# Graph hops that gather with one f32 product per item, with build steps placed inside the hops

## The chip, the cores and the metric

One core of a Trainium2 chip runs the whole program. The metric is device time in microseconds from start to end of one execution; smaller is better. The engines are TensorE (PE, matmul; its weight loads are listed as PEld and its sequencer as PEldq), VectorE (DVE), ScalarE (ACT), GpSimd (POOL) and SyncE (SP, which issues DMAs).

## The reference, cut to what matters

A graph has 3125 nodes with 128 features and 100000 edges, sorted by destination. Layer 0 is an attention layer with five hops; layer 1 is three graph convolutions.

```python
# layer 0: a[e, head] is the softmax share of edge e at its destination node
f = feat0
for _ in range(HOP):                                   # HOP = 5
    msg = f[src] * a[:, :, None]
    agg = jax.ops.segment_sum(msg, dst, num_segments=n)
    f = (1.0 - ALPHA) * agg + ALPHA * feat0
...
# layer 1: three times
h = x @ W
out = jax.ops.segment_sum(h[src_a] * norm[:, None], dst_a, num_segments=n) + b
```

Two things are computed around the change. A *hop* reads the row of each edge's source node, weighs it by the edge's eight head shares, and sums it at the destination. The *adjacency* for layer 1 is built once as a dense table in DRAM, `adj`, from the edges' weights.

## The kernel before, in words

Nodes are cut into 25 buckets of 125. The edges of one (destination bucket) or of one (source bucket, destination bucket) pair are cut into items of up to 128 edges; four items make a group.

**Hop 0** runs over 51 iterations of four groups. For each group SP loads rows that an earlier stage left in DRAM, VectorE makes the destinations' one-hot (L1402) and weighs the rows (L1449), and TensorE adds them up per bucket in PSUM with two products for each item, one for the rows and one for the weights' sum (L1062, L1065). From iteration 8 (`BUILD_FROM`) on, one **build step** goes with each group. A step is four items of the adjacency: VectorE writes a place factor (L1409) and four key factors (L1413), TensorE multiplies them into cells in PSUM bank 7 (`build_cells`, L1049), VectorE adds the cells to a running sum (`build_sums`, L1425), and SP stores four rows of it to `adj` (`store_step`, L690). There are 352 steps; 172 are done in hop 0, and **180 in loops of their own behind it** (L1294, L1706, L1983).

Beside hop 0 GpSimd writes one record for each edge to DRAM, sorted by bucket pair (L869). Behind the 180 steps comes the **record stage**: GpSimd gathers the records, 128 items at a time, eleven times (L880), and TensorE turns them (`turn_records`, L1071). It leaves the shares in `ex_it`, the destinations in `dst_c`, and the sources, as bf16, in DRAM (`ids_d`). GpSimd's first gather waits for all record DMAs and for the sums of hop 0.

**Hops 1 to 4** each run over 352 groups, in 44 iterations of eight. The rows of the current node table `na` stay in SBUF, and a group goes like this:

- SP loads the sources of two groups at a time, the same row into all 125 partitions (L717), into a ring of four.
- VectorE compares them with the partition's number, which gives the source one-hots in bf16 (`compare_sources`, L1455).
- TensorE gathers: one-hot times the rows of the item's source bucket, into bank 7 (`gather_items`, L1112). The table is kept as three bf16 parts, so an item takes three bf16 matmuls that add up in PSUM.
- VectorE weighs bank 7 into `msg` (`weigh`, L1472) and makes the next group's destination one-hot (`dst_onehots`, L1462).
- TensorE scatters: destination one-hot times `msg`, added to the destination bucket in banks 0 to 6 (L1103), in f32. An f32 product shows as two weight loads and two matmuls.

TensorE's order is written out in `cell_pass` (L1084): for group k it loads the bucket numbers of gather k+1 and of scatter k into registers (`cell_regs`, L553, four at a time), waits for the weigh of group k, issues gather k+1, then scatter k. There is one bank for the gathered rows, so gather k+1 cannot start before weigh k has read it.

Between hops VectorE adds `feat0` to the banks (`hop_sums`, L1977), ScalarE and VectorE **split** the new table into its three bf16 parts (`split_parts`, L985, and `split_rest`, L1488), and TensorE clears banks 0 to 6 (L1041). The feed-forward part of layer 0 and the three convolutions follow.

Semaphores set all of the order. Every engine's and SP's instructions run in the order in which they are written, so whatever stands behind a wait waits too.

Of the kernel before, what the change touches and what calls it, by code (L numbers as in the profile page):

```python
# [12 lines left out]
P = 128  # L13
# [40 lines left out]
BUILD_FROM = 8  # L54
BUILD_AFTER = STEPS - (ITERS - BUILD_FROM) * SLOTS
# [5 lines left out]
assert SLOTS == 2 * BSLOTS and BG * NB * WN <= BANK and BUILD_AFTER % SLOTS == 0 < BUILD_AFTER  # L61
# [16 lines left out]
MASKS = 12  # L78
# [10 lines left out]
PARTS_F = 3  # L89
# [5 lines left out]
HALF = ITEMS // 2  # L95
assert ITEMS % 2 == 0 and HALF <= BANK
# [17 lines left out]
def gnn_stack(nc, a, out):  # L114
    ctx = ExitStack()
    with ctx:
# [38 lines left out]
        src_it = sb("src_it", [P, KB * P], I32)  # L155
        dloc = sb("dloc", [P, KB * P])
        w_it = sb("w_it", [P, KB * P])
# [6 lines left out]
        pidx = sb("pidx", [P, 1])  # L164
        dump_at = sb("dump_at", [P, 1])
# [135 lines left out]
        def tail_part(n):  # L301
# [16 lines left out]
        idb = gap_f[:, 0:PK * P // 2].bitcast(BF16).rearrange("p (k e) -> p k e", e=P)  # L318
        dst_rows = gap_f[:, PK * P // 2:PK * P // 2 + 2 * P].rearrange("p (s e) -> p s e", s=2)
        ids_at = PK * P // 2 + 2 * P  # L320
        ids = gap_f[:, ids_at:ids_at + PRING * LOAD * P // 2].bitcast(BF16).rearrange("p (s n) -> p s n", s=PRING)
        assert ids_at + PRING * LOAD * P // 2 <= L // 2 + 1
        dst_c = raw[:, 0:PITEMS]
        cell_row = x_sb.rearrange("p b f -> p (b f)")[0:1, 0:2 * PITEMS].bitcast(I32)
        split_at = 2 * NB * F
        split = U[:, split_at:split_at + PARTS_F * NB * F // 2].bitcast(BF16).rearrange("p (k b f) -> p k b f", k=PARTS_F, f=F)
        assert 2 * PITEMS <= NB * F and PARTS_F * NB * F // 2 <= (NB + 1) * F + NB * BN
        rec_in = ga_flat[:, 0:2 * P * REC].rearrange("p (s e c) -> p s e c", s=2, c=REC)
        msg = ga_flat[:, 0:PRING * G * F].rearrange("p (s g f) -> p s g f", s=PRING, g=G)
        src_t = ga_flat[:, PRING * G * F:PRING * G * F + PRING * LOAD * P // 2].bitcast(BF16).rearrange(  # L330
            "p (s i e) -> p s i e", s=PRING, e=P)
        rest = ga_flat[:, 0:BANKS * BANK].rearrange("p (s n) -> p s n", s=BANKS)
# [200 lines left out]
        def group_of(s, r, k):  # L533

            return r * PSTEPS + ((s - 1) * PGROUPS + k)

        def load_of(s, r, q):

            return r * PRING + ((s - 1) * PLOADS + q)
# [1557 lines left out]
```

## Time and profile before

| | us |
|---|---|
| median of 2 runs (8714.96 to 8715.48) | 8715.22 |
| the profiled execution, its own time | 8704.12 |
| its span, first to last instruction | 8702.4 |

| engine | busy us | share of the span |
|---|---|---|
| PE (matmul) | 6495.1 | 75% |
| PEld (weight load) | 5400.2 | 62% |
| DVE | 4864.4 | 56% |
| POOL | 1744.7 | 20% |
| ACT | 406.5 | 5% |

The mean granted clock of TensorE is 0.811 of 2.4 GHz; in a stretch it is mostly 0.50 (1.2 GHz) or 1.00. Shares are means over stages with different limits, so each stage has to be read by itself. Matmuls are pipelined, their ends are modelled, and a busy PE is not a PE at its peak. "issue" is idle time in which the engine waited for nothing that the profile shows. Times in rows count from the span's start.

### The profile page before, as it was taken

What the parts mean: (1) busy time and instruction counts of PE and PEld (TensorE: products, weight loads), DVE (VectorE), ACT (ScalarE), POOL (GpSimd) and SP (SyncE); (2) the same over time, 40 slices, a digit from 0 to 9 for tenths busy, and PEclk for the clock granted to TensorE, in tenths of its full rate; (3) what the DMA queues carried; (4) which work ended last, traced back from release to release, by engine and by line L of the source; (5) the groups of instructions that cost most, each with busy time, mean ns of one, the idle gap of its engine ahead of it and who ended that gap; (6) DMA issues with size and microseconds to landing.
All of it is one profiled execution on the core that took longest, in us unless ns stands there. A gap on an engine that the chain in (4) does not pass through costs nothing.

```text
span 8702.4 us, 162184 instructions
## 1 busy us (share of the span) xinstructions
PE 6495.1 (75%) x41703; PEld 5400.2 (62%) x41704; DVE 4864.4 (56%) x9329; ACT 406.5 (5%) x1487; POOL 1744.7 (20%) x1671
## 2 busy tenths in 40 slices
PE   4455464599994445888888888888888888888599
PEld 2344353599994444666666666666666666666499
DVE  7888577788887776444444444444444444444411
ACT  0111111100000000000000000000000000000100
POOL 0677575477774000000000000000000000000000
PEclk9565555555555556999999999999999999999899
DMA  2344643234432222111111111101111111111276
GB/s 59 116 138 133 131 141 98 57 106 106 107 105 68 62 62 79 39 39 39 39 39 37 39 39 39 39 37 39 39 39 39 38 39 39 39 39 39 78 271 241
DMA packets 546072, 646.43 MB, mean 74 GB/s; under 512 B 84553, under 2 KB 393084, under 8 KB 536029
## 3 DMA queue, kind: packets, MB, share of 16 engines
q1 hardware_dynamic: 475380, 520.58, 18.4%
q0 software_dynamic: 67216, 120.62, 5.1%
q10 hardware_dynamic: 3418, 4.48, 0.2%
q8 instruction: 32, 0.52, 0.0%
q14 instruction: 26, 0.21, 0.0%
HBM read 487.75 MB, written 158.90 MB: 74 GB/s over the span
## 4 chain that ended last, share of the span: by engine, by line
PE 67%; issue 14%; DVE 11%; POOL 3%; DMA 2%; DVEq 1%; ACT 1%; SPq 1%; POOLq 0%; ACTq 0%; PEldq 0%; PEld 0%
PE ps L1112 27%; PE ps L1103 17%; PE ps L1049 7%; PE ps L1065 6%; PE ps L1358 5%; POOL U L821 3%; DVE gap L1425 3%; PE ps L1062 2%; PE ps L1227 1%; PE ps L1220 1%; DVE U L1933 1%; DVE U L1905 1%; DMA U<-tab_he,stage 1%; DVE gap L1413 1%; DVE gap L1541 1%
## 5 line engine op out<-in xcount | busy, mean ns | idle before, releaser
L1112 PE MATMUL ps<-U 125*128 x16896 | 2354.7, 228 | 821.0 <-issue 792.5
L1112 PEld LDWEIGHTS ps<-U 125*128 125x128 bf16 x16896 | 1628.5, 96 | 1626.0 <-issue 1085.6
L1472 DVE TENSOR_TENSOR U<-ps,ex_it 128x512 f32<-128x512 f32 x1408 | 976.5, 694 | 2538.2 <-PE ps L1112 2538.2
L1103 PE MATMUL ps<-U 128*125 128x128 f32 x11264 | 1608.4, 284 | 0.0
L1103 PEld LDWEIGHTS ps<-U 128*125 128x125 f32 x11264 | 1346.6, 187 | 45.1 <-issue 0.2
L1049 PE MATMUL ps<-gap 128*128 128x125 f32 x2816 | 695.2, 425 | 402.2 <-DVE gap L1425 402.2
L821 POOL DMA_INDIRECT U<-tab_he,stage x806 | 843.7, 1047 | 525.0 <-issue 243.5
L1462 DVE TENSOR_TENSOR U<-raw,iota_p 128x500 f32<-128x500 f32 x1408 | 944.4, 671 | 0.0
L1049 PEld LDWEIGHTS ps<-gap 128*128 128x128 f32 x2816 | 635.1, 330 | 448.8 <-issue 448.8
L869 POOL DMA_INDIRECT rec_d<-ex_it,stage x806 | 847.4, 1051 | 245.5 <-issue 228.8
L1425 DVE SCALAR_TENSOR_TENSOR gap<-gap,U,ps 128x125 f32<-128x125 f32 x1408 | 487.2, 346 | 273.8 <-PE ps L1049 100.4
L1065 PE MATMUL ps<-U 128*125 128x128 f32 x1632 | 628.1, 489 | 0.0
L1227 PE MATMUL ps<-U 125*128 x1632 | 402.4, 424 | 217.3 <-ACT U L930 216.4
L1227 PEld LDWEIGHTS ps<-U 125*128 125x128 f32 x1632 | 345.5, 313 | 274.9 <-issue 274.9
L1220 PE MATMUL ps<-ident,U 128*125 128x128 f32 x816 | 225.6, 428 | 334.8 <-DVE U L1402 319.7
L1062 PEld LDWEIGHTS ps<-w_it,U 128*125 128x125 f32 x1632 | 444.5, 333 | 5.8 <-issue 5.8
L1065 PEld LDWEIGHTS ps<-U 128*125 128x125 f32 x1632 | 443.1, 332 | 0.0
L1220 PEld LDWEIGHTS ps<-ident,U 128*125 128x125 f32 x816 | 186.4, 313 | 370.1 <-DVE U L1402 347.8
L1413 DVE TENSOR_SCALAR gap<-iota_p,U,raw 128x125 f32<-128x125 f32 x1408 | 388.7, 356 | 0.0
L1062 PE MATMUL ps<-w_it,U 128*125 x1632 | 344.3, 280 | 4.2 <-DVE U L1449 4.2
L1455 DVE TENSOR_SCALAR U<-gap,pidx 125x1024 bf16<-125x1024 bf16 x704 | 339.1, 482 | 0.1
L1402 DVE TENSOR_TENSOR U<-dloc,iota_p 128x500 f32<-128x500 f32 x409 | 282.5, 691 | 86.1 <-DMA U<-edge_fe 53.4
(323 smaller groups left out, 3604.4 us busy)
## 6 DMA issues: line engine op xcount, KB each, us to landing
gap<-ids_d SPq DMA_DIRECT2D x704, 250.0 KB
adj<-gap SPq DMA_DIRECT2D x1408, 64.0 KB
edge_fe<-U SPq DMA_DIRECT2D x204, 256.0 KB, 2.5
U<-edge_fe SPq DMA_DIRECT2D x204, 256.0 KB
ex_it<-adj SPq DMA_DIRECT2D x30, 1600.0 KB, 6.1
U<-adj SPq DMA_DIRECT2D x30, 1600.0 KB, 6.1
fe_a<-adj SPq DMA_DIRECT2D x15, 1600.0 KB, 6.1
U<-tab_he,stage POOLq DMA_INDIRECT x806
```

Of the source, the lines that this page charges most:

```text
L821: pool.indirect_dma_start(to[:, k, j, :], None, table, bass.IndirectOffsetOnAxis(ap=stage[:, k, j:j + 1], axis=0)).then_inc(got[k], 16)
L869: pool.indirect_dma_start(rec_d, bass.IndirectOffsetOnAxis(ap=stage[:, k, j:j + 1], axis=0), recs[:, k, j, :], None).then_inc(got[k], 16)
L1049: mm = nc.tensor.matmul(cells_at(j), hot_p[:, k % BSLOTS, j, :], prod[:, k % BSLOTS, j, :], start=True, stop=True)
L1062: nc.tensor.matmul(ps[0:BN, bass.ds(b + W_SUMS, 1)], hot[:, k, j, :], w_it[:, bass.ds(r * PER_ITER + (k * G + j), 1)], start=False, stop=F ...
L1065: mm = nc.tensor.matmul(ps[0:BN, bass.ds(b * F, F)], hot[:, k, j, :], ga[:, k, j, :], start=False, stop=False, skip_group_check=True)
L1103: mm = nc.tensor.matmul(ps[0:BN, bass.ds(b * F, F)], dst_hot[:, k % PRING, j, :], msg[:, k % PRING, j, :], start=False, stop=False, skip_g ...
L1112: mm = nc.tensor.matmul(bank(7)[:, j * F:(j + 1) * F], src_t[0:BN, k // 2, k % 2 * G + j, :], split[0:BN, n, bass.ds(b, 1), :].rearrange(" ...
L1220: t = nc.tensor.transpose(bank(k % 2)[0:BN, j * P:(j + 1) * P], hot[:, k, j, :], ident[:])
L1227: mm = nc.tensor.matmul(bank(2 + k % 2)[:, j * F:(j + 1) * F], hot_t[:, k % 2, j, :], nb_pad[0:BN, bass.ds(b, 1), :].rearrange("p b f -> p ...
L1425: ins = v.scalar_tensor_tensor(out=win_acc[:, u, j, 0:CELL], in0=before, scalar=win_same[:, bass.ds(win_item(t, r, k, j), 1)], in1=cells_a ...
L1462: v.tensor_tensor(dst_hot[:, (k + ahead) % PRING], dst_c[:, bass.ds(r * (PSTEPS * G) + (k + ahead) * G, G)].unsqueeze(2).to_broadcast([P, ...
L1472: v.tensor_tensor(msg[:, k % PRING].rearrange("p g (h d) -> p (g h) d", h=HEADS), bank(7).rearrange("p (x d) -> p x d", d=HD), by, ALU.mul ...
```

## The change

1. The three bf16 parts and the split are gone. The gather is one f32 product for each item, with source one-hots in f32, in a ring of two loads instead of four.
2. The source one-hots move from VectorE to ScalarE, as two dependent activations: |source - partition|, then relu(1 - that).
3. The bucket numbers are interleaved in `cell_row` (three small loads instead of one), and TensorE reads eight for each group with one register load.
4. Builds begin at iteration 7 of hop 0 (176 steps there). The loops of 180 steps are gone; the other 176 steps go into hops 1 to 4, one for each eight groups. In group 4 (`CELL_AT`) TensorE builds cells in bank 7 between weigh 4 and gather 5, and ScalarE copies them out (`cells_kept`). VectorE does the rest in pieces: the place factor in group 0, key factors in groups 1 and 2, sums in groups 5 and 6.
5. SP stores a step's four rows in the next iteration, behind the first of its four loads of sources.

Some buffers move; the ids rings now lie in spare places of other tiles.

```diff
-BUILD_FROM = 8
-BUILD_AFTER = STEPS - (ITERS - BUILD_FROM) * SLOTS
+BUILD_FROM = 7
+STEPS_0 = (ITERS - BUILD_FROM) * SLOTS
+SRING = 2
+CELL_AT = 4
...
+            def load_ids(s, r, q):
+                sp.wait_ge(src_hots, load_of(s, r, q) + 1)
+                sp.dma_start(ids[q][0:BN, :], ids_d[bass.ds(r * (PRING * LOAD * P) + q * LOAD * P, LOAD * P)]
+                             .partition_broadcast(BN)).then_inc(loaded[q], 16)
+
             for s in range(1, HOPS):
-                with sp.Fori(0, PITERS) as r:
-                    for q in range(PRING):
-                        sp.wait_ge(src_hots, load_of(s, r, q) + 1)
-                        sp.dma_start(ids[0:BN, q, :], ids_d[bass.ds(r * (PRING * LOAD * P) + q * LOAD * P, LOAD * P)]
-                                     .partition_broadcast(BN)).then_inc(loaded[q], 16)
+                for r0, r1 in cut(0, 1, PITERS):
+                    with sp.Fori(r0, r1) as r:
+                        load_ids(s, r, 0)
+                        if s > 1 or r0:
+                            store_step(r * BG + (STEPS_0 + (s - 1) * PITERS - 1) * BG, step_of(s, r) + 1, 1)
+                        for q in range(1, PRING):
+                            load_ids(s, r, q)
+            store_step((STEPS - 1) * BG, STEPS + 1, 1)
...
-            act.wait_ge(built, 1)
...
+            def compare_sources(s, r, q, ahead=0):
+
+                use = (q + ahead) % PRING
+                to = src_t[0:BN, use % SRING].rearrange("p i e -> p (i e)")
+                act.wait_ge(loaded[use], r * 16 + 16 * (ITERS + (s - 1) * PITERS + 1 + (q + ahead) // PRING))
+                act.wait_ge(gathered, 2 * load_of(s, r, q + ahead) + 2)
+                nc.scalar.activation(to, ids[use][0:BN, :], ACT.Abs, bias=below[0:BN, 0:1]).then_inc(src_apart, 1)
+                act.wait_ge(src_apart, load_of(s, r, q + ahead) + 1)
+                nc.scalar.activation(to, to, ACT.Relu, bias=ones[0:BN, 0:1], scale=-1.0).then_inc(src_hots, 1)
+
+            for s in range(1, HOPS):
+                compare_sources(s, 0, 0)
+                for r0, r1 in cut(0, PITERS - 1, PITERS):
+                    with act.Fori(r0, r1) as r:
+                        for q in range(PRING):
+                            if q == PRING - 1:
+                                act.wait_ge(cell_sums, step_of(s, r) + 1)
+                                nc.scalar.copy(cells_kept, bank(7, BG * CELL)).then_inc(cells_out, 1)
+                            if not (r0 and q == PRING - 1):
+                                compare_sources(s, r, q, 1)
...
             def cell_pass(s):
-                pe.wait_ge(split_done, BANKS * s)
                 pe.wait_ge(src_hots, (s - 1) * PLOADS + 1 + PRING)
-                gather_items(0, cell_regs(pe, 0))
+                gather_items(0, cell_regs(pe, 2 * PITEMS, G))
...
-                            of = None if last else cell_regs(pe, i + G)
-                            to = cell_regs(pe, i + PITEMS)
+                            v_ = cell_regs(pe, i + G, G) if last else cell_regs(pe, i, 2 * G)
 
                             pe.wait_ge(weighted, group_of(s, r, k) + 1)
+                            if k == CELL_AT:
+                                build_cells(step_of(s, r), 0)
+                                scatter_items(s, r, k, v_[-G:])
+                                pe.wait_ge(cells_out, r + ((s - 1) * PITERS + 1))
                             if not last:
                                 if k % 2:
                                     pe.wait_ge(src_hots, load_of(s, r, (k + 1) // 2) + (1 + PRING))
-                                gather_items((k + 1) % PSTEPS, of)
+                                gather_items((k + 1) % PSTEPS, v_[0:G])
+                            if k != CELL_AT:
+                                scatter_items(s, r, k, v_[-G:])
...
             def gather_items(k, cells):
 
                 for j, b in enumerate(cells):
-                    for n in range(PARTS_F):
-                        mm = nc.tensor.matmul(bank(7)[:, j * F:(j + 1) * F], src_t[0:BN, k // 2, k % 2 * G + j, :],
-                                              split[0:BN, n, bass.ds(b, 1), :].rearrange("p b f -> p (b f)"),
-                                              start=(n == 0), stop=(n == PARTS_F - 1))
+                    mm = nc.tensor.matmul(bank(7)[:, j * F:(j + 1) * F], src_t[0:BN, k // 2 % SRING, k % 2 * G + j, :],
+                                          na[0:BN, bass.ds(b, 1), :].rearrange("p b f -> p (b f)"), start=True, stop=True)
                 mm.then_inc(gathered, 1)
...
+            def build_in_hop(s, r, k):
+
+                item = r * BG + (STEPS_0 + (s - 1) * PITERS) * BG
+                if k == 0:
+                    place_factor(item, 0)
+                if k in (1, 2):
+                    ins = key_factors(item, 0, (2 * k - 2, 2 * k - 1))
+                    if k == 2:
+                        ins.then_inc(prod_ready, 1)
+                if k == CELL_AT + 1:
+                    dve.wait_ge(cells_out, r + ((s - 1) * PITERS + 1))
+                    dve.wait_ge(acc_out[1], r * (16 * BG) + 16 * BG * (STEPS_0 // BSLOTS + (s - 1) * PITERS + 1))
+                if k in (CELL_AT + 1, CELL_AT + 2):
+                    lanes = (0, 1) if k == CELL_AT + 1 else (2, 3)
+                    add_cells(item, step_of(s, r), 1, 1, lanes, lambda j: cells_kept[:, j * CELL:(j + 1) * CELL])
...
             def cell_pass(s):
-                compare_sources(s, 0, 0)
                 dst_onehots(s, 0, 0)
...
-                            if k % 2 == 0 and not (r0 and k == PSTEPS - 2):
-                                compare_sources(s, r, k // 2, 1)
                             weigh(s, r, k)
                             if not (r0 and k == PSTEPS - 1):
                                 dst_onehots(s, r, k, 1)
+                            build_in_hop(s, r, k)
...
-            with dve.Fori(0, BUILD_AFTER // SLOTS) as r:
-                for k in range(SLOTS):
-                    build_factors(STEPS - BUILD_AFTER, r, k)
-                    build_sums(STEPS - BUILD_AFTER, r, k - 1)
-            build_sums(STEPS, 0, -1)
-            dve.sem_inc(built, 1)
+            build_sums(ITERS, -1)
...
             for n in range(1, HOPS):
-                split_rest(n - 1)
                 cell_pass(n)
```

## Rows read from the trace of the kernel before

**Rows 1.** The page's chain that ended last, shares of the span by line.

```profile
PE ps L1112 27%; PE ps L1103 17%; PE ps L1049 7%; PE ps L1065 6%; PE ps L1358 5%; POOL U L821 3%; DVE gap L1425 3%; PE ps L1062 2%; PE ps L1227 1%; PE ps L1220 1%; DVE U L1933 1%; DVE U L1905 1%; DMA U<-tab_he,stage 1%; DVE gap L1413 1%; DVE gap L1541 1%
```

**Rows 2.** Windows: stretch, length, busy us (instructions) of PE, PEld, DVE, ACT, POOL; PEclk, DMA, GB/s.

```profile
2900.00:3000.00 100.00, 48.78 (x192) 42.53 (x192) 73.17 (x213) 0.00 (x0) 0.00 (x0) 0.50 0.21 63
...
5000.00:5100.00 100.00, 82.52 (x611) 64.29 (x611) 44.34 (x76) 0.00 (x0) 0.00 (x0) 1.00 0.10 39
```

**Rows 3.** Timeline of one group in hop 2: start, duration, instructions, idle before.

```profile
5000.41 1.65 PE L1112 MATMUL ps<-U 125*128 x12 [0.88 <-issue]
...
5001.95 1.14 PE L1103 MATMUL ps<-U 128*125 128x128 f32 x8
5002.21 0.69 DVE L1472 TENSOR_TENSOR U<-ps,ex_it 128x512 f32<-128x512 f32 x1 [2.19 <-PE ps L1112]
5002.82 0.67 DVE L1462 TENSOR_TENSOR U<-raw,iota_p 128x500 f32<-128x500 f32 x1
5003.40 0.48 DVE L1455 TENSOR_SCALAR U<-gap,pidx 125x1024 bf16<-125x1024 bf16 x1
...
5003.68 1.67 PE L1112 MATMUL ps<-U 125*128 x12 [0.59 <-issue]
5004.05 0.26 SPq L717 DMA_DIRECT2D gap<-ids_d  x1
```

**Rows 4.** Line 553's instructions in 5002.45 to 5003.3: ns min/median/max, first and last start.

```profile
L553 PEldq TENSOR_LOAD <-U x2: 330/332/335, 5002.5 to 5003.0; - x2
```

**Rows 5.** Timeline from the end of hop 1 into hop 2.

```profile
4593.89 3.16 PE L1041 MATMUL ps<-zeros 1*128 1x512 bf16 x7 [3.97 <-DVE U L1977]
...
4602.76 1.82 PE L1112 MATMUL ps<-U 125*128 x12 [5.70 <-DVE U L1455]
4604.83 0.69 DVE L1472 TENSOR_TENSOR U<-ps,ex_it 128x512 f32<-128x512 f32 x1 [1.73 <-PE ps L1112]
...
4605.68 1.76 PE L1112 MATMUL ps<-U 125*128 x12 [1.10 <-DVE U L1472]
...
4607.28 2.07 PE L1103 MATMUL ps<-U 128*125 128x128 f32 x8
```

**Rows 6.** Windows of 4 us at the start of hop 2, columns as in rows 2.

```profile
4606.00:4610.00 4.00, 4.00 (x27) 3.58 (x26) 1.78 (x4) 0.00 (x0) 0.00 (x0) 0.54 0.18 69
4610.00:4614.00 4.00, 3.40 (x27) 2.63 (x27) 1.28 (x2) 0.00 (x0) 0.00 (x0) 1.00 0.18 68
```

**Rows 7.** Timeline of a build step in hop 0, VectorE and SP.

```profile
2306.42 1.11 DVE L1413 TENSOR_SCALAR gap<-iota_p,U,raw 128x125 f32<-128x125 f32 x4
...
2307.05 1.88 SPq L690 DMA_DIRECT2D adj<-gap  x4
...
2308.27 0.35 DVE L1425 SCALAR_TENSOR_TENSOR gap<-gap,U,ps 128x125 f32<-128x125 f32 x1 [0.16 <-DVE gap L1425]
```

**Rows 8.** Timeline of the record stage: GpSimd's first gather, and TensorE behind it.

```profile
2747.15 1.00 POOL L880 DMA_INDIRECT U<-rec_d,pair_t  x1 [2.17 <-DMA rec_d<-ex_it,stage]
...
3385.05 1.91 PE L1079 MATMUL ps<-ident,U 128*128 128x128 f32 x8
...
3391.15 0.94 POOL L880 DMA_INDIRECT U<-rec_d,pair_t  x1 [0.98 <-PE ps L1082]
...
3395.93 1.98 PE L1079 MATMUL ps<-ident,U 128*128 128x128 f32 x8
```

**Rows 9.** Timeline ahead of hop 1: the first ids loads, and the first gather.

```profile
3426.95 15.06 SPq L717 DMA_DIRECT2D gap<-ids_d  x7
...
3435.18 1.75 PE L1112 MATMUL ps<-U 125*128 x12 [6.21 <-DVE U L1455]
```

**Rows 10.** ScalarE's groups by line and shape: busy us, mean ns, idle before.

```profile
L1022 ACT ACTIVATE U<-ps,b_ff 128x500 f32<-128x500 f32 x24 | 16.3, 678 | 24.7 <-PE ps L1316 24.2
...
L954 ACT ACTIVATE ex_it<-U 128x2176 f32<-128x2176 f32 x3 | 6.1, 2019 | 69.1 <-DVE U L1940 69.1
```

**Rows 11.** Windows of a quarter us around that ids load: the last with data (PEclk, DMA, GB/s).

```profile
5007.00:5007.25 0.25, 1.00 0.14 49
```

More of the change, by code:

```diff
@@ L60 @@
 RING = 5
-assert SLOTS == 2 * BSLOTS and BG * NB * WN <= BANK and BUILD_AFTER % SLOTS == 0 < BUILD_AFTER
+assert SLOTS == 2 * BSLOTS and BG * NB * WN <= BANK
 assert WINDOWS * WN == N_NODES and WPB * WN == BN
@@ L95 @@
 HALF = ITEMS // 2
+assert STEPS == STEPS_0 + (HOPS - 1) * PITERS and STEPS_0 % 2 == 0
 assert ITEMS % 2 == 0 and HALF <= BANK
@@ L164, in gnn_stack @@
         pidx = sb("pidx", [P, 1])
+        below = sb("below", [P, 1])
         dump_at = sb("dump_at", [P, 1])
@@ L700, in _ @@
                     load_group(r, k)
[L701 removed]
+                    store_step(win_item(first, r, k), r * SLOTS + (first + k + 2), k % BSLOTS)
+            for k in range(SLOTS):
+                t = STEPS_0 - SLOTS + k
+                store_step(t * BG, t + 2, k % BSLOTS)
             sp.wait_ge(cell_out, 16 * 2)
[L704 to L708 removed]
+            own = cell_row[0:1, 0:2 * PITEMS].rearrange("o (g c) -> o g c", c=2 * G)
+            of_src, of_dst = (cell_d[n * PITEMS:(n + 1) * PITEMS].rearrange("(o g c) -> o g c", o=1, c=G) for n in range(2))
+            sp.dma_start(own[:, 0:PGROUPS - 1, 0:G], of_src[:, 1:PGROUPS, :]).then_inc(cell_in, 16)
+            sp.dma_start(own[:, :, G:2 * G], of_dst).then_inc(cell_in, 16)
+            sp.dma_start(cell_row[0:1, 2 * PITEMS:2 * PITEMS + G], of_src[:, 0, :]).then_inc(cell_in, 16)
             sp.wait_ge(dst_rows_ready, 2 * PK)
@@ L1293, in _ @@
             sum_groups(BUILD_FROM, ITERS)
-            with pe.Fori(0, BUILD_AFTER // SLOTS) as r:
-                for k in range(SLOTS):
-                    build_cells(STEPS - BUILD_AFTER, r, k)
             turn_records()
-            pe.wait_ge(cell_in, 16)
+            pe.wait_ge(cell_in, 16 * 3)
             pe.wait_ge(rec_kept_a, 2 * PK)
@@ L1425, in build_sums, with add_cells @@
+            def add_cells(item, step, u, before_u, lanes, of):
+                for j in lanes:
+                    before = win_acc[:, u, j - 1, 0:CELL] if j else win_acc[:, before_u, BG - 1, 0:CELL]
                     ins = v.scalar_tensor_tensor(
-                        out=win_acc[:, u, j, 0:CELL], in0=before, scalar=win_same[:, bass.ds(win_item(t, r, k, j), 1)],
-                        in1=cells_at(j), op0=ALU.mult, op1=ALU.add)
+                        out=win_acc[:, u, j, 0:CELL], in0=before, scalar=win_same[:, bass.ds(item + j, 1)],
+                        in1=of(j), op0=ALU.mult, op1=ALU.add)
```

174 lines of the change are left out of this document (69 added, 105 removed).

## The prediction

> **What bounds the kernel now.** I read the chain that ended last first, because it names the two lines to look at: the matmuls of the gather (L1112) hold 27% of the span, those of the scatter (L1103) 17%, and the build matmuls (L1049) 7% [rows 1]. The windows by stage say where those lines live: a build stretch behind hop 0 where TensorE is under half busy at half clock, and hops at the full clock where TensorE is busy 82% and VectorE 44% [rows 2]. So there are two stages to price, and in neither is TensorE full.
>
> In the hops the timeline gives one group [rows 3]: twelve bf16 gather matmuls, 1.65 us; eight f32 scatter matmuls (four products, two instructions each), 1.14 us; then nothing on TensorE for about 0.55 us, although the weigh that the next gather waits for (started 5002.21, 0.69 us) was done at 5002.90 and the gather starts at 5003.68. What is late is TensorE's own sequencer: it makes two loads of bucket numbers of 0.33 us each, at 5002.5 and 5003.0 [rows 4], and only after it has issued the scatter, which TensorE goes on running until about 5003.1. Where those loads are hidden, at the start of a hop, the gather starts 0.16 us after the weigh ends (4604.83 + 0.69 to 4605.68) [rows 5]. The third thing to see is that a bf16 pair of weight load and matmul takes 1.65 / 12 = 0.137 us and an f32 pair, with twice the work in it, 1.14 / 8 = 0.142 us [rows 3]: the pace is that of instructions, not of columns. Hop 1 runs from its first gather at 3435.18 [rows 9] to 4589.9 (4593.89 less 3.97 of idle) [rows 5], 1154.7 us for 352 groups: 3.28 us a group, 26.2 us for eight.
>
> **The build behind hop 0.** 180 steps disappear there. The record stage starts now at 3385.05. What is late next is GpSimd: its scatter of records ends just ahead of its first record gather at 2747.15, and such a gather lands 4.78 us after its start (3391.15 to 3395.93) [rows 8]. What it had waited for there was its own record DMAs, not hop 0. So the stage can start at 2751.9, and **633 us** go. The four steps that hop 0 gains (about 2 us each, by a 2.07 us burst at the same clock [rows 5]), their stores, and the three small loads of the interleaved bucket numbers lie in front of that same GpSimd wait and cost nothing; without that cover they would cost some 10 us.
>
> **The split.** Between hops TensorE waits today from 4589.9 to 4602.76; without the split the next gather needs the hop sums and the clear (4593.89 + 3.16), and starts near 4597.2 [rows 5]: 5.5 us, three times, **16.5 us**. Ahead of hop 1 the ids become the chain: issue at 3426.95, about 3.0 us to land, 2.45 us of compare, 0.16: 3432.6 instead of 3435.18 [rows 9], **2.6 us**.
>
> **One group of a hop.** Gather and scatter are each eight f32 pairs. I take for the gather the row of the scatter, same shapes and one dynamic address each: 1.14 us to its end, about 0.99 us of TensorE before the next burst can follow. I bound it by a fifth less, since an f32 pair then takes hardly less than a bf16 one, and by the 1.65 us of today. The chain gather to gather is then 1.14 + 0.15 (5002.06 to 5002.21) + 0.69 weigh + 0.16 = **2.14 us**; the two bursts fill 1.98 of it, and the sequencer has 16 pairs and one load of eight numbers instead of two of four. The sequencer had issued four f32 products between 5001.95 and 5002.5, so eight take some 1.2 us; with one load and the 0.35 us from the end of a load to the gather that is about 1.9 us. A load of eight has no row: 0.33 us as for four, or 0.66 if it costs by the number, which makes 2.2 and adds 0.1. I take 2.14, since it is one instruction.
>
> VectorE has 1.3 us of weigh and one-hot in each group, and in five of eight groups a piece of a build step: one place factor (0.67, as the one-hot), two times two key factors (1.11 for four), two times two sums (0.35 and 0.15 for the link to the next) [rows 7]. Only the groups with sums, 1.3 + 1.0, pass 2.14: 2.3 us, twice in eight.
>
> **The build step in the hop.** In group 4 it puts eight more f32 pairs (0.99 us) into bank 7 between weigh and gather, and since the gather must wait for ScalarE's copy of the cells, the scatter goes first and no longer covers the next weigh: the group takes 0.69 + 0.16 + 0.99 + 0.99 + 1.14 + 0.15 = 4.1 us. The copy itself (some 0.7 us) is covered by that scatter.
>
> **The new wait, which I expect to show.** SP now waits, behind its first ids load of eight groups, for the sums of the step before, and queued behind that wait are four stores and then the other three ids loads. The sums end in group 6, about when the weigh of group 7 starts. From there: 0.15 to wake, 1.88 us for four stores [rows 7], then the load, whose issue starts at 5004.05 in the old hops and whose data have stopped by about 5007.1 [rows 3, 11], so 3.0 us: ids at +5.1 us. Then the compare on ScalarE. No row has Abs; ScalarE's activations take 0.678 us for 500 columns and 2.019 us for 2176 [rows 10], on that line 1.10 us for 1024. Bounds: the slope alone, 0.82 us, and two of the shorter, 1.36. Two of them, dependent, 0.15 between: 2.35 us, against 0.48 us for the one instruction on VectorE today [rows 3]. Ids compared at +7.6 us, gather at +7.7. Without it the gather of that group (the second after) would start at 0.69 + 0.16 + 2 x 2.14 = +5.1. So 2.6 us of stall for every eight groups. The other compares have two groups, 4.3 us, for 2.35 us of work, and their ids are there.
>
> The Trainium skill, ScalarE: Activation LUTs, Rules for kernel authors, advises VectorE and not ScalarE for simple functions such as relu; that speaks against this move, and with VectorE's 0.48 us in the chain eight groups would take 1.9 us less, and the whole some 330 us. The rows agree: 0.48 us there, 1.10 us an instruction here.
>
> **Sum for eight groups**, from weigh 7 to weigh 7: 7.7 to the late gather, 1.29 to its weigh, 2 x 2.14 = 4.28, 4.1 with the build, 2 x 2.3 = 4.6: **22.0 us** against 26.2. Of such there are 4 x 44 = 176: 4.2 x 176 = **740 us**. The first groups of a hop at half clock (about 2 us) and the missing stall of a hop's first eight groups (2.6 us) cancel.
>
> Together 633 + 16.5 + 2.6 + 740 = 1392 us. The profiled execution took 8704.1 us, so 7312; the median of the runs is 11 us longer, so **about 7320 us**. Two per cent, about what a measurement of this kernel can tell from no change, is 174 us.
>
> **Rivals.**
> 1. *The ids are hidden* (chance 0.15). If the stores cost SP less than I count, or a load lands sooner, the stall goes: 8 x 2.14 + 2.0 + 0.3 = 19.5 us, 440 us less: **6880**. For it: the queue was never late before. Against: the four stores and three loads are in one queue, and the rows give each its time.
> 2. *The clock stays low* (0.07, the one on the slower side). The place is the hops: only f32 products are left there, and the all-f32 stretch behind hop 0 ran at 1.2 GHz throughout [rows 2]. At that level eight f32 pairs take about 1.8 us (4607.28, 2.07 us to its end, overlapped by the next) [rows 5], a group 3.6, eight with the build 8 x 3.6 + 1.8 + 1.2 = 31.8 us, 9.8 more than forecast in each of 176: **9040**. It decides from the point where the hops run mostly at 1.2 GHz; at half the time there the gain is still about 500 us. Against it: at a hop's start TensorE was busy without a gap in a stretch with a mean clock of 0.54, and was at 2.4 GHz afterwards [rows 6], and at 1.2 GHz the f32 bursts leave no gap, because each outlasts the 1.0 us of the weigh.
> 3. *One f32 product is no cheaper than three bf16 ones* (0.03). If work and not instructions set the pace, with four passes in place of three the gather would take 1.65 x 4 / 3 = 2.2 us, a group 2.2 + 0.15 + 0.69 + 0.16 = 3.2, eight about 8 x 3.2 + 3 = 28.6: **8480**. Against it stands the scatter's row, four f32 products in 1.14 us. The Trainium skill, FP8 and Floating Point Precision, states that true FP32 makes four passes through the array; by that rule alone this rival would hold, and the trace differs: 0.285 us for an f32 product, 0.41 us for three bf16 ones.
> 4. *The compare becomes the bound* (0.05). At twice my price on ScalarE, four compares of 4.9 us, the cells' copy and the late ids make about 26 us for eight groups, as now: **8030**, from the build stage alone.
>
> My own case has 0.70, and its unknowns (pair 0.107 to 0.14 us, load of eight, Abs, landing of ids up to 0.5 us later) put eight groups between 20.5 and 23.5 us: 7060 to 7590. To hold 8 in 10 the range takes in rival 1 below and goes part of the way towards rival 4 above: **6860 to 7720**. Faster by over 2% needs less than 8541 us: my case, rivals 1, 3 and 4, less some room for what I have not seen: 0.89. Rival 2 is the slower side: 0.06. Within 2%: 0.05.
>
> **What would show it.** The build stage gone and the record stage at about 2752 us, hop 1 at about 2798. Hops of about 966 us, clock 1.00, eight f32 gather pairs of about 1.1 us. In each eight groups one TensorE idle time of about 2.6 us that ends with ScalarE's second activation, behind an ids load that follows four stores on SP; and one group of about 4.1 us. If that idle time is missing, rival 1; if the clock is 0.50 in the hops, rival 2; if the gather bursts take over 1.6 us, rival 3. The prediction is wrong in its mechanism if the record stage does not wait for GpSimd, or if the hops are paced by VectorE.

## The result, and the profile after

The changed kernel takes 7992.38 us (median of two runs, 7986.86 to 7997.89) against 8715.22: a ratio of 0.9171, 95% interval 0.9131 to 0.921. It is faster, as forecast, but the time lies above the range. The profiled execution has a span of 7985.0 us and a mean granted clock of 0.775, less than the 0.811 of before.

Half of the story went as planned. The timeline of the record stage and of the start of hop 1 (start, duration, instructions, idle before):

```profile
2746.50 0.99 POOL L900 DMA_INDIRECT U<-rec_d,pair_t  x1 [2.12 <-DMA rec_d<-ex_it,stage]
...
2750.82 1.95 PE L1104 MATMUL ps<-ident,U 128*128 128x128 f32 x8 [124.55 <-DMA U<-rec_d,pair_t]
...
2791.94 0.69 SPq L725 DMA_DIRECT2D item_cols<-ids_d  x2
...
2792.67 0.73 SPq L725 DMA_DIRECT2D U<-ids_d  x2
...
2797.48 1.15 ACT L1019 ACTIVATE U<-item_cols,below 125x1024 f32<-125x1024 bf16 x1 [6.33 <-DMA item_cols<-ids_d]
...
2800.37 2.07 PE L1142 MATMUL ps<-U 125*128 x8 [5.88 <-ACT U L1021]
```

The first transposes start at 2750.82 instead of 3385.05 [rows 8], behind GpSimd's own scatter, and hop 1 starts at 2800.37 instead of 3435.18 [rows 9]. That is 634.8 us, all in front of the hops. The record stage alone gives 634.2 of it; from there to the first gather it is 49.55 us, hardly less than the 50.13 of before: the first sources, issued at 2791.94, are used only 5.54 us later.

The hops themselves gave little. The sums behind the last one end at 7377.6, so the four take 4577.2 us, and from one set of stores to the next between 3900 and 5100 us eight groups take 25.85 us on average (the step from one hop to the next left out), against 26.2 before. The waits from 4000 to 5000 us say what took the gain (who waits for whom, us in total, times, longest):

```profile
ACT U L1019 <- DMA item_cols<-ids_d: 369.3, 38, 10.2
...
PE ps L1142 <- ACT U L1021: 174.4, 39, 4.9
```

Once in every eight groups ScalarE waits for sources, and then TensorE waits 4.5 us for ScalarE. One such place, in the timeline of hop 2, to be set beside [rows 3]:

```profile
5001.53 1.97 SPq L695 DMA_DIRECT2D adj<-gap  x4
5001.67 0.69 DVE L1512 TENSOR_TENSOR U<-ps,ex_it 128x512 f32<-128x512 f32 x1 [0.30 <-DVE gap L1448]
...
5003.76 0.34 SPq L725 DMA_DIRECT2D item_cols<-ids_d  x1
...
5004.35 0.81 SPq L725 DMA_DIRECT2D U<-ids_d  x2
...
5004.97 1.15 PE L1142 MATMUL ps<-U 125*128 x8 [0.32 <-DVE U L1512]
...
5008.92 1.15 ACT L1019 ACTIVATE U<-item_cols,below 125x1024 f32<-125x1024 bf16 x1 [9.69 <-DMA item_cols<-ids_d]
5010.10 1.15 ACT L1021 ACTIVATE U<-U,ones 125x1024 f32<-125x1024 f32 x1
...
5011.40 1.73 PE L1142 MATMUL ps<-U 125*128 x8 [4.40 <-ACT U L1021]
...
5012.92 1.91 PE L1135 MATMUL ps<-U 128*125 128x128 f32 x8
5013.28 0.69 DVE L1512 TENSOR_TENSOR U<-ps,ex_it 128x512 f32<-128x512 f32 x1 [5.23 <-PE ps L1142]
...
5016.12 0.69 DVE L1512 TENSOR_TENSOR U<-ps,ex_it 128x512 f32<-128x512 f32 x1 [1.05 <-PE ps L1142]
...
5018.36 0.69 DVE L1512 TENSOR_TENSOR U<-ps,ex_it 128x512 f32<-128x512 f32 x1 [0.96 <-PE ps L1142]
...
5022.40 0.69 DVE L1512 TENSOR_TENSOR U<-ps,ex_it 128x512 f32<-128x512 f32 x1 [2.76 <-PE ps L1142]
```

Two things are to be seen. The load that SP issues behind the four stores, at 5003.76, is used at 5008.92, 5.16 us later; the gather follows its two activations. And the bursts behind the idle time take 1.73 and 1.91 us, where the undisturbed ones take 1.15 and 1.04. Windows of the same stretch (length, busy us of PE, PEld, DVE, ACT, POOL; then granted clock, DMA share, GB/s) show why:

```profile
5008.00:5010.00 2.00, 0.00 (x0) 0.00 (x0) 0.06 (x1) 1.08 (x1) 0.00 (x0) 1.00 0.32 117
5010.00:5012.00 2.00, 0.60 (x4) 0.60 (x5) 0.00 (x0) 1.97 (x3) 0.00 (x0) 0.95 0.33 127
5012.00:5014.00 2.00, 2.00 (x12) 2.00 (x11) 0.72 (x2) 1.44 (x2) 0.00 (x0) 0.50 0.33 127
5014.00:5016.00 2.00, 2.00 (x14) 2.00 (x14) 1.07 (x3) 0.00 (x0) 0.00 (x0) 0.69 0.04 16
```

TensorE did nothing from about 5007.0 to 5011.4; its clock fell to 1.2 GHz when the late burst had begun, and was back at 2.4 GHz by 5016. This iteration is one of the milder ones. In another the clock fell while TensorE still stood idle, and the whole late gather ran at 1.2 GHz (its row, and two windows):

```profile
4026.29 2.07 PE L1142 MATMUL ps<-U 125*128 x8 [4.65 <-ACT U L1021]
```

```profile
4024.00:4026.00 2.00, 0.00 (x0) 0.00 (x0) 0.00 (x0) 1.97 (x2) 0.00 (x0) 0.84 0.33 128
4026.00:4028.00 2.00, 1.71 (x8) 1.72 (x9) 0.00 (x0) 1.97 (x3) 0.00 (x0) 0.50 0.33 128
```

Between 4000 and 5000 us, 35 of the 39 late gathers take 2.0 us or more. The mean clock there is 0.89.

The question for the experiments is therefore: is it the order on SP that makes this load late, is it the transfers, is it ScalarE, and what does the clock add?

### The profile page after: what moved, and what is told of

Read it like the earlier page. It is cut to its first block, busy times and chain, and to the rows that moved or that the text cites. A ratio compares the mean times of both kernels' runs of the same rounds, so it can differ in the third digit from the quotient of the medians.

```text
span 7985.0 us, 137914 instructions
## 1 busy us (share of the span) xinstructions
PE 5703.8 (71%) x36071; PEld 5263.7 (66%) x36072; DVE 4508.5 (56%) x8569; ACT 2078.5 (26%) x3015; POOL 1739.8 (22%) x1672
## 4 chain that ended last, share of the span: by engine, by line
PE 35%; DMA 15%; DVE 13%; issue 13%; POOL 11%; ACT 6%; SPq 5%; DVEq 1%; POOLq 0%; ACTq 0%; PEldq 0%; PEld 0%
PE ps L1142 13%; DMA item_cols<-ids_d 11%; PE ps L1135 10%; POOL rec_d L889 7%; PE ps L1384 5%; SPq L695 4%; POOL U L841 4%; DVE U L1502 3%; DVE gap L1448 3%; PE ps L1073 3%; ACT U L1019 3%; ACT U L1021 3%; PE ps L1256 2%; DMA rec_d<-ex_it,stage 1%; PE ps L1249 1%
## 5 line engine op out<-in xcount | busy, mean ns | idle before, releaser
L1142 PE MATMUL ps<-U 125*128 x11264 | 1853.7, 315 | 1157.7 <-ACT U L1021 781.6
L1142 PEld LDWEIGHTS ps<-U 125*128 125x128 f32 x11264 | 1597.7, 219 | 1365.6 <-issue 1351.4
L1135 PEld LDWEIGHTS ps<-U 128*125 128x125 f32 x11264 | 1520.2, 207 | 0.9 <-issue 0.9
L1502 DVE TENSOR_TENSOR U<-item_cols,iota_p 128x500 f32<-128x500 f32 x1408 | 944.3, 671 | 0.4 <-ACT item_cols L1011 0.3
L1019 ACT ACTIVATE U<-item_cols,below 125x1024 f32<-125x1024 bf16 x352 | 404.7, 1150 | 1948.9 <-DMA item_cols<-ids_d 1713.3
L1021 ACT ACTIVATE U<-U,ones 125x1024 f32<-125x1024 f32 x704 | 809.6, 1150 | 22.9
L1256 PE MATMUL ps<-U 125*128 x1632 | 407.7, 428 | 213.6 <-ACT U L950 212.7
L1073 PE MATMUL ps<-gap 128*128 128x125 f32 x2816 | 538.4, 352 | 15.4
L1019 ACT ACTIVATE U<-U,below 125x1024 f32<-125x1024 bf16 x352 | 402.1, 1142 | 544.5 <-PE ps L1142 544.4
L1256 PEld LDWEIGHTS ps<-U 125*128 125x128 f32 x1632 | 350.2, 317 | 271.7 <-issue 271.7
L1087 PEld LDWEIGHTS ps<-item_cols,U 128*125 128x125 f32 x1632 | 444.4, 333 | 6.0 <-issue 6.0
L1090 PEld LDWEIGHTS ps<-U 128*125 128x125 f32 x1632 | 442.9, 332 | 0.0
L1087 PE MATMUL ps<-item_cols,U 128*125 x1632 | 344.3, 280 | 4.3 <-DVE U L1497 4.3
```

Source lines behind the costliest of these rows:

```text
L1019: nc.scalar.activation(to, ids[use][0:BN, :], ACT.Abs, bias=below[0:BN, 0:1]).then_inc(src_apart, 1)
L1021: nc.scalar.activation(to, to, ACT.Relu, bias=ones[0:BN, 0:1], scale=-1.0).then_inc(src_hots, 1)
L1073: mm = nc.tensor.matmul(cells_at(j), hot_p[:, u, j, :], prod[:, u, j, :], start=True, stop=True)
L1087: nc.tensor.matmul(ps[0:BN, bass.ds(b + W_SUMS, 1)], hot[:, k, j, :], w_it[:, bass.ds(r * PER_ITER + (k * G + j), 1)], start=False, stop=F ...
L1090: mm = nc.tensor.matmul(ps[0:BN, bass.ds(b * F, F)], hot[:, k, j, :], ga[:, k, j, :], start=False, stop=False, skip_group_check=True)
L1135: mm = nc.tensor.matmul(ps[0:BN, bass.ds(b * F, F)], dst_hot[:, k % PRING, j, :], msg[:, k % PRING, j, :], start=False, stop=False, skip_g ...
```

## The experiments

All times are medians of four runs; the kernel before took 8703.83 us beside the first four, 8706.79 beside the next four and 8702.07 beside the last two. Line numbers shift a little from kernel to kernel.

**The stores last.** All four loads of an iteration go ahead of the wait and the stores.

```diff
-                        load_ids(s, r, 0)
+                        for q in range(PRING):
+                            load_ids(s, r, q)
                         if s > 1 or r0:
                             store_step(r * BG + (STEPS_0 + (s - 1) * PITERS - 1) * BG, step_of(s, r) + 1, 1)
-                        for q in range(1, PRING):
-                            load_ids(s, r, q)
```

> All four loads of sources of an iteration stand on SP ahead of the wait for the sums and the four stores. Theory (the order on SP makes the first load behind the stores late, TensorE idles 4.4 us for it and comes back at 1.2 GHz): the idle time that ends with ScalarE's second activation goes, the clock stays at 1.00, eight groups take the sum of the undisturbed ones, 2.24 + 4.04 + 2.34 + 2.33 + 2.36 + 3 x 2.25 = 20.1 us against 25.4, and 5.3 x 176 = 940 us go: about 7050 us. Rival A (the loads are slow because transfers disturb each other, whatever the order): the landings stay near 5 us but there is room for them, so the same 7050; this run does not tell it apart. Rival B (the compares on ScalarE pace the hops): four compares of 2.33 us and the copy stay, the idle time stays: 7900 to 8000 us. Rival C (the lower clock belongs to f32 hops and not to the idle time): clock stays near 0.9, about 21.3 us, 7270 us.

Measured: 6944.92 us (6939.65 to 6953.01), 0.7978 of before [0.7964, 0.7991]. Eight groups take 19.90 us on average, and the clock in the hops is 0.98 to 1.00. The timeline of hop 2:

```profile
5015.07 2.05 SPq L695 DMA_DIRECT2D adj<-gap  x4
...
5017.74 0.90 SPq L725 DMA_DIRECT2D item_cols<-ids_d  x2
...
5019.63 1.15 ACT L1018 ACTIVATE U<-U,below 125x1024 f32<-125x1024 bf16 x1 [2.40 <-PE ps L1141]
...
5022.84 1.15 PE L1141 MATMUL ps<-U 125*128 x8
```

ScalarE now waits for TensorE (2.40 us), no longer for sources, and TensorE, within the hop, for nothing but the weigh. Rivals B and C fall. The time is 105 us below the 7050 expected: the groups summed to 20.1 us and took 19.9, and the iteration of the kernel after that was taken as the model had 25.4 us where the average is 25.85 us.

**One load ahead of the stores.** The wait stays in its place; only the load moves in front of the four stores (its wait for a free ring place goes ahead of the wait for the sums).

```diff
                 sp.wait_ge(acc_ready, done)
+                if ahead:
+                    ahead()
                 for j in range(BG):
...
                         if s > 1 or r0:
-                            store_step(r * BG + (STEPS_0 + (s - 1) * PITERS - 1) * BG, step_of(s, r) + 1, 1)
-                        for q in range(1, PRING):
+                            sp.wait_ge(src_hots, load_of(s, r, 1) + 1)
+                            store_step(r * BG + (STEPS_0 + (s - 1) * PITERS - 1) * BG, step_of(s, r) + 1, 1,
+                                       lambda: load_ids(s, r, 1, False))
+                        else:
+                            load_ids(s, r, 1)
+                        for q in range(2, PRING):
                             load_ids(s, r, q)
```

> SP keeps the wait for the sums where it is, but issues the first load that stood behind the stores right after the wait, ahead of the four stores; the other two loads stay behind them. Theory, with the stores' 2.1 us of issue and the neighbouring loads as the two terms: the load is issued 0.2 us after the last sum, alone, lands 3.0 us later, ids compared at +5.6, and TensorE waits 0.3 to 0.6 us instead of 4.4: about 20.5 us for eight groups, 7130 us. Rival A (the data of the stores slow the load to 5.2 us): the load lands at +5.4, gather at +7.9, 2.5 us of idle time are left and some of the low clock: 22.6 to 23.2 us, 7500 to 7600 us. Rival B (ScalarE's compares pace it): 7900 to 8000 us.

Measured: 7162.99 us (7156.04 to 7165.56). The timeline:

```profile
5017.58 0.30 SPq L728 DMA_DIRECT2D item_cols<-ids_d  x1
...
5018.07 2.10 SPq L697 DMA_DIRECT2D adj<-gap  x4
...
5021.63 1.15 ACT L1026 ACTIVATE U<-item_cols,below 125x1024 f32<-125x1024 bf16 x1 [6.35 <-DMA item_cols<-ids_d]
...
5024.12 1.15 PE L1149 MATMUL ps<-U 125*128 x8 [0.69 <-ACT U L1028]
```

The idle time is 0.69 us, with four stores right behind the load: their data don't slow it as rival A said. But the load is used 4.05 us after its issue, not 3.0.

**A load by itself.** Order and stores as in the kernel after; the two later loads wait until ScalarE has finished its first activation on the first.

```diff
-            def load_ids(s, r, q):
-                sp.wait_ge(src_hots, load_of(s, r, q) + 1)
+            def load_ids(s, r, q, behind=None):
+                if behind is None:
+                    sp.wait_ge(src_hots, load_of(s, r, q) + 1)
+                elif behind != q:
+                    sp.wait_ge(src_apart, load_of(s, r, behind) + 1)
...
-                        for q in range(1, PRING):
-                            load_ids(s, r, q)
+                        sp.wait_ge(src_hots, load_of(s, r, 2) + 1)
+                        load_ids(s, r, 1, 1)
+                        load_ids(s, r, 2, 1)
+                        load_ids(s, r, 3)
```

> The order of the kernel after stays: wait, four stores, three loads. But the second and third of these loads wait until ScalarE has finished the first activation on the first load, so that no load is issued next to it. Theory (loads issued back to back share the transfer engines, so that the first one takes 5.2 us instead of 3.0): the first one lands 3.0 us after its issue, TensorE idles about 2.2 us instead of 4.4, eight groups take 23.2 us or up to 1.3 less where the clock stays up: 7400 to 7600 us, and up to 170 us more if the later load is now late itself. Rival A (the stores' data slow it, or 5 us is what such a load takes behind stores): the first activation still starts 5.2 us after the issue, 7950 to 8160 us.

Measured: 7786.87 us (7782.3 to 7798.71), above the 7400 to 7770 of the theory and below the 7950 of rival A. The timeline says what each got wrong:

```profile
5004.47 0.35 SPq L728 DMA_DIRECT2D item_cols<-ids_d  x1
...
5008.36 1.15 ACT L1024 ACTIVATE U<-item_cols,below 125x1024 f32<-125x1024 bf16 x1 [8.83 <-DMA item_cols<-ids_d]
...
5009.68 0.81 SPq L728 DMA_DIRECT2D U<-ids_d  x2
...
5010.85 1.15 PE L1147 MATMUL ps<-U 125*128 x8 [3.56 <-ACT U L1026]
...
5014.81 1.15 ACT L1024 ACTIVATE U<-U,below 125x1024 f32<-125x1024 bf16 x1 [4.11 <-DMA U<-ids_d]
...
5017.29 1.15 PE L1147 MATMUL ps<-U 125*128 x8 [1.00 <-ACT U L1026]
```

Alone, a load is used 3.89 us after its issue; two issued together, with no store in flight, 5.13 us after theirs. The windows of the two cases (columns as above):

```profile
5005.50:5006.00 0.50, 0.50 (x6) 0.50 (x6) 0.50 (x2) 0.00 (x0) 0.00 (x0) 1.00 0.33 119
5006.00:5006.50 0.50, 0.50 (x7) 0.50 (x6) 0.21 (x1) 0.00 (x0) 0.00 (x0) 1.00 0.33 127
...
5007.50:5008.00 0.50, 0.00 (x0) 0.00 (x0) 0.50 (x3) 0.00 (x0) 0.00 (x0) 1.00 0.06 21
5008.00:5008.50 0.50, 0.00 (x0) 0.00 (x0) 0.34 (x2) 0.14 (x1) 0.00 (x0) 1.00 0.00 0
...
5011.00:5011.50 0.50, 0.50 (x5) 0.50 (x6) 0.00 (x0) 0.00 (x0) 0.00 (x0) 1.00 0.33 123
5011.50:5012.00 0.50, 0.50 (x7) 0.50 (x6) 0.00 (x0) 0.00 (x0) 0.00 (x0) 1.00 0.20 49
5012.00:5012.50 0.50, 0.50 (x6) 0.50 (x5) 0.34 (x1) 0.00 (x0) 0.00 (x0) 0.73 0.19 66
5012.50:5013.00 0.50, 0.50 (x5) 0.50 (x4) 0.50 (x2) 0.00 (x0) 0.00 (x0) 0.50 0.19 61
```

So the 5.16 us of the kernel after have two parts beyond the 3.0 of the forecast. The data of the lone load stop soon after 5007.5, about 3.1 us after the issue, and ScalarE starts only at 5008.36: some 0.7 to 0.8 us pass between the last data and the reader. And neighbours add 1.27 us (5.16 less 3.89): the load alone moves 119 to 127 GB/s, while two together fall to 49 to 66 GB/s. The theory's mechanism holds; its 3.0 us does not, and the later load was late in its turn (the second idle time, 1.00 us).

**One activation.** The absolute difference is left out of the compare.

```diff
-                nc.scalar.activation(to, ids[use][0:BN, :], ACT.Abs, bias=below[0:BN, 0:1]).then_inc(src_apart, 1)
-                act.wait_ge(src_apart, load_of(s, r, q + ahead) + 1)
-                nc.scalar.activation(to, to, ACT.Relu, bias=ones[0:BN, 0:1], scale=-1.0).then_inc(src_hots, 1)
+                nc.scalar.activation(to, ids[use][0:BN, :], ACT.Relu, bias=ones[0:BN, 0:1], scale=-1.0).then_inc(src_hots, 1)
```

> The compare on ScalarE is one activation instead of two: the absolute difference is left out, so that what TensorE gathers with is not a one-hot, and the times of everything else stay. Theory (the late load and then the two activations stand in the chain once per eight groups): the late gather starts 1.17 us earlier, idle 3.2 instead of 4.4 us, 24.2 us for eight groups: 7785 us, down to 7560 where the clock falls for a shorter time. Rival B (ScalarE's four compares pace the hops): four times 1.17 us go, 20.7 us: 7165 us. Rival D (the compare is hidden, another wait ends last): 7990 us.

Measured: 7685.55 us (7675.58 to 7701.69), within the theory's 7560 to 7785. 307 us over 176 are 1.74 us of each eight groups: 1.17 of the activation, and 0.57 that I put down to less time at the low clock (mean 0.92 in 4000 to 5000 us). Rival B wanted four activations and 7165; rival D no change.

**The idle time filled.** Sixteen f32 products of a constant tile stand ahead of the wait for the late sources.

```diff
+                            if k == 1:
+                                for j in range(16):
+                                    nc.tensor.matmul(bank(7)[:, 0:P], ident[:], ident[:], start=True, stop=True)
                             if not last:
```

> The kernel after, with sixteen f32 products of a constant tile by itself, whose result is overwritten unread, put on TensorE in front of the wait for the late sources: about 4.0 of the 4.4 us of idle time are filled, and the wait itself stays. Theory (the idle time lets TensorE's clock fall to 1.2 GHz, and the bursts behind it then take 1.73 and 1.91 us instead of 1.15 and 1.04): the clock in the hops goes to 1.00, the first bursts behind the wait take 1.15 and 1.04, about 1.3 us of each eight groups go: 7760 us. Rival E (the clock falls for another reason, as the f32 products themselves): clock stays near 0.9 and the time is 7990 us, or up to 100 more where the fillers outlast the wait.

Measured: 7695.15 us (7685.73 to 7699.47), and the wait is as long as ever. The timeline:

```profile
5021.07 3.84 PE L1126 MATMUL ps<-ident 128*128 128x128 f32 x32
...
5025.57 1.15 PE L1145 MATMUL ps<-U 125*128 x8 [0.67 <-ACT U L1021]
...
5026.56 1.04 PE L1138 MATMUL ps<-U 128*125 128x128 f32 x8
```

With TensorE kept busy through the wait, the bursts behind it take 1.15 and 1.04 us, all 39 late gathers between 4000 and 5000 us take 1.15 us, the mean clock there is 0.99, and 297 us are gone: useless work made the kernel 1.69 us faster in each eight groups. Rival E falls; the f32 products alone don't lower the clock.

**Two register loads, on the version with the stores last.**

```diff
-v_ = cell_regs(pe, i + G, G) if last else cell_regs(pe, i, 2 * G)
+v_ = cell_regs(pe, i + G, G) if last else [*cell_regs(pe, i, G), *cell_regs(pe, i + G, G)]
```

> The version with the stores last (6945 us), with the eight bucket numbers of a group read by two register loads of four instead of one of eight. A load of eight takes 0.59 us here, one of four took 0.33 before, so some 0.25 to 0.35 us more of TensorE's sequencer in each of 1408 groups. Theory (the chain of gather and weigh paces the groups, and the loads are covered by the bursts and the weigh): 0 to 0.1 us a group, 6945 to 7090 us. Rival F (the sequencer paces the groups, as it did before): 0.25 to 0.35 us a group, 7300 to 7440 us.

Measured: 6998.24 us (6993.84 to 7001.79), 53 us more: 0.04 us a group. In the kernel after one load of eight takes 0.59 us (line 558's loads in 4990 to 5040; ns min/median/max):

```profile
L558 PEldq TENSOR_LOAD <-U x15: 587/591/596, 4992.7 to 5037.8; - x15
```

So the price goes nearly by the number: 0.59 us lies near the upper of the forecast's two values, 0.66. But it is nearly hidden: the sequencer no longer sets the pace.

**No cells, on the version with the stores last.** The waits on the copy go with it.

```diff
-                            if k == CELL_AT:
-                                build_cells(step_of(s, r), 0)
-                                scatter_items(s, r, k, v_[-G:])
-                                pe.wait_ge(cells_out, r + ((s - 1) * PITERS + 1))
...
-                            if k != CELL_AT:
-                                scatter_items(s, r, k, v_[-G:])
+                            scatter_items(s, r, k, v_[-G:])
...
-                            if q == PRING - 1:
-                                act.wait_ge(cell_sums, step_of(s, r) + 1)
-                                nc.scalar.copy(cells_kept, bank(7, BG * CELL)).then_inc(cells_out, 1)
...
-                    dve.wait_ge(cells_out, r + ((s - 1) * PITERS + 1))
```

> The version with the stores last, without the cells in the hops: TensorE's eight matmuls of a build step and ScalarE's copy are left out, so that the last 176 steps of the adjacency are wrong; factors, sums and stores stay. Theory (the group with the build takes 4.04 us because the cells stand between weigh and gather and the scatter no longer covers a weigh): that group goes to 2.25 us, 1.8 us x 176 = 315 us: 6630 us. Rival G (only the matmuls' own 1 us counts, since the copy is covered): 0.99 x 176 = 174 us, 6770 us.

Measured: 6616.85 us (6615.57 to 6618.98): 328 us, 1.86 us of each eight groups. The theory's 1.8 holds, and the build costs nearly twice what its own matmuls take. Factors, sums and stores ran on.

**One activation, on the version with the stores last.** The edit is that of the other run with one activation.

> The version with the stores last, with one activation in the compare instead of two (the absolute difference is left out, so that what TensorE gathers with is not a one-hot). Theory (with the loads in time the compare on ScalarE is hidden): 6945 us, within 0.5 per cent. Rival B (ScalarE's compare is part of the pace): up to 1.17 us for each eight groups or more, 6740 us or less.

Measured: 6944.66 us (6941.82 to 6953.4), no change. The same edit was worth 307 us where the sources came late.

**All partitions.** Half-microsecond windows show a lone load at a DMA share of 0.32 to 0.33, about five of sixteen engines (0.31). Here each load goes to 128 partitions instead of 125; the order is that of the kernel after.

```diff
-                sp.dma_start(ids[q][0:BN, :], ids_d[bass.ds(r * (PRING * LOAD * P) + q * LOAD * P, LOAD * P)]
-                             .partition_broadcast(BN)).then_inc(loaded[q], 16)
+                sp.dma_start(ids[q], ids_d[bass.ds(r * (PRING * LOAD * P) + q * LOAD * P, LOAD * P)]
+                             .partition_broadcast(P)).then_inc(loaded[q], 16)
```

> The kernel after, in its order, with each load of sources written into all 128 partitions instead of 125. While one load of 125 is under way the DMA share is 0.31 to 0.34, which is five of the sixteen engines, at 119 to 127 GB/s. Theory (a load of 125 partitions runs on five engines only, and one of 128 on all sixteen, so its data take about 0.7 us instead of 2.3, and neighbours finish as fast): the load behind the stores is used 2.2 to 2.8 us after its issue instead of 5.16, TensorE idles about 2 us instead of 4.4, and the clock falls for a shorter time or not at all: 21.5 to 23.2 us for eight groups, 7230 to 7530 us. Rival H (the 2 KB that all partitions read from one place in DRAM, or the issue, limits the load): DMA share and latency stay, 7990 us.

Measured: 7557.57 us (7555.18 to 7560.13), just above the theory's range, and far from rival H. The timeline, and two windows with the loads under way:

```profile
5011.92 0.35 SPq L725 DMA_DIRECT2D item_cols<-ids_d  x1
...
5015.48 1.15 ACT L1019 ACTIVATE U<-item_cols,below 125x1024 f32<-125x1024 bf16 x1 [8.17 <-DMA item_cols<-ids_d]
...
5017.96 1.47 PE L1142 MATMUL ps<-U 125*128 x8 [2.94 <-ACT U L1021]
```

```profile
5013.50:5014.00 0.50, 0.50 (x7) 0.50 (x6) 0.47 (x1) 0.00 (x0) 0.00 (x0) 1.00 0.55 156
...
5015.50:5016.00 0.50, 0.00 (x0) 0.00 (x0) 0.50 (x3) 0.50 (x1) 0.00 (x0) 1.00 0.99 373
```

The share goes up to 0.99 and the rate to 373 GB/s, three times the old. But the first load is used 3.56 us after its issue, more than the 2.2 to 2.8 expected: about 0.9 us pass before its first data, as with the lone load, and while its neighbours join, the rate is only 156 to 217 GB/s. The Trainium skill, DMA: Bandwidth & Descriptors, Why a DMA increments its semaphore by 16 and not by 1, states that such a transfer runs on the largest number of engines up to sixteen that divides its outer dimension; by that 125 gives five and 128 sixteen, and the two shares agree.

**All partitions, on the version with the stores last.** The same edit.

> The version with the stores last, with the loads into 128 partitions as well. Theory (the loads are hidden there): only the first load of each hop is in the way, at most 2 us in each of four: 6935 to 6945 us. Rival (transfers still cost something in the hops, at TensorE or VectorE): more than 1 per cent of difference, 6870 us or less.

Measured: 6942.44 us (6940.36 to 6943.08), no change against 6944.92: in time is in time.

## Why the prediction was wrong

**Right:** the record stage at 2751.9 (2750.82), hop 1 at 2798 (2800.37), so the 633 us of the build stage came. The 16.5 us between the hops came too: from the end of TensorE's work in hop 1 to the first gather of hop 2 it is 7.1 us (3936.32 to 3943.38) instead of 12.8. Of the 2.6 us ahead of hop 1 only about 0.6 came (50.13 less 49.55), for the reason given next. The f32 gather at 1.14 us (1.15). The group of the build at 4.1 (5018.36 to 5022.40, 4.04). The compare, 2.35 us from start to end (2.33). The place and the cause of the new wait: one idle time for every eight groups that ends with ScalarE's second activation, behind an ids load that follows four stores. Plain groups took 2.24 instead of 2.14 us, which is small. Two slips in the forecast's sums change little: the compare ahead of hop 1 is put at 2.45 us and elsewhere at 2.35, and its own terms put hop 1 at about 2799.4, not 2798.

**The step that failed** is "then the load, whose issue starts at 5004.05 in the old hops and whose data have stopped by about 5007.1 [rows 3, 11], so 3.0 us: ids at +5.1 us". They were used at +7.25 (5001.67 to 5008.92). The lone-load run shows both parts of the miss: the end of the data is not the moment at which a waiting engine starts (about 0.9 us more, 3.89 in all), and the old hop's load travelled alone, while this one has two others issued right behind it (1.27 us more). The forecast's own row could not show the first, since nothing in the old hop waited for that load; the second was in view, because the text itself said that three loads are queued behind the stores, and the loads that the old kernel issued back to back ahead of hop 1 fall from 125 to 39 GB/s there (windows of 1 us, 3428 to 3431). The same 3.0 us failed ahead of hop 1, where the first of four loads was used 5.54 us after its issue. TensorE's idle time came to 4.40 us instead of 2.6. The Trainium skill, DMA: Bandwidth & Descriptors, Anatomy of one DMA, describes DMAs issued by GpSimd, not by SP as here: it puts about 2 us of fixed cost on each, most of it behind the last byte. It could have been a hint of the first part, but not of its size: of SP's loads here some 0.7 to 0.8 us lie behind the last data.

**The term that was missing** is the clock. The forecast expected 1.00 in the hops, and rival 2 asked only whether f32 products lower it. What lowered it was the idle time that the forecast itself had predicted. Between 4000 and 5000 us of the kernel after, the 39 idle times last 4.2 to 4.9 us, and each late gather behind them takes 1.87 to 2.07 us; with the fillers, 0.4 to 1.2 us of idle time remain, and every one takes 1.15. In between the bursts differ from one iteration to the next: with idle times of 2.5 to 3.1 us (all partitions) the late gathers take from 1.15 to 2.07 us. The run with the fillers prices the low clock at 1.69 us for each eight groups.

Term by term for the iteration shown, weigh 7 to weigh 7: the late gather at +9.73 instead of 7.7 (2.0 more), then its weigh (0.6) and the next group (0.7) by the clock, and 0.1 elsewhere: 25.4 instead of 22.0. On average it is 25.85 us, since most iterations lose more to the clock (1.69 us by the fillers, 1.3 in the one shown), and (25.85 - 22.0) x 176 = 678 us; the miss is 7992 - 7320 = 672.

Rival 1 (no stall, 19.5 us, 6880) was the alternative that the order of SP decides: with the stores last it happens, at 19.90 us and 6945. The whole then closes: 633 + 19 + (26.2 - 19.9) x 176 = 1761 us against 8704 - 6945 = 1759 measured beside each other. Rival 3 is refuted by the gather's row, rival 4 by the run with the stores last: the same compares, no wait for them.

The Trainium skill, ScalarE: Activation LUTs, Rules for kernel authors, advises VectorE for simple functions such as relu. No run here moves the compare back to VectorE, but the two runs with one activation show when its length counts: an activation less is worth 307 us with the sources late, and nothing with the sources in time.

**The best version** is the one with the stores last: 6944.92 us, 0.7978 of before, while the kernel after stands at 0.9171 of it. What its cells in the build group still cost is 328 us.

## What to carry to other kernels

A transfer is late or in time by what stands ahead of it in its queue: put loads that somebody needs soon ahead of waits and stores that nobody waits for, even when the total is the same. Take a load's latency from a row in which an engine waits for it, with as many neighbours as it will have; the end of its data is too early. And when a forecast contains an idle time of TensorE, price the bursts behind it at the low clock as well.

## What was not expected of the hardware

- A load into 125 partitions used about a third of the DMA engines, and one into 128 all of them: 123 against 373 GB/s.
- Two loads of 125 x 2 KB in flight together moved less in sum than one alone for 2 to 2.5 us: 49 to 66 GB/s against 119 to 127. It was the same without any stores nearby, so the stores are not the cause; with 128 partitions the dip was there too (156 to 217 against 344 to 373). What causes it stays open.
- The clock did not fall at the same point of every idle time. In the iteration shown it was still 1.00 up to 5011.5 and 0.50 from 5012 on, when TensorE was already at work again; in the one at 4026 it had fallen before the work came back, and stayed low until 4032.
- A register load of eight numbers takes 0.59 us against 0.33 for four [rows 4].
